# Turning V by VectorE and block transfers, and scoring wide rows in steps of 512 keys, in a fused attention and ternary layer

## What is computed

```
y = x * rsqrt(mean(x*x) + eps) * rms_w
q, k, v = split(y @ w_in.T)              # 32 q heads, 8 k heads, 8 v heads
q, k = rope(q), rope(k)
qk = q @ k.T / 8, causal mask, softmax
y = (attn @ v) @ w_out.T
x = layernorm(x + (x + y))
x_q = ternary(x); w = ternary(weight) + rram_variation
out = layernorm(x + x_q @ w.T)
```

## Time and profile before

| | us |
|---|---|
| median of 3 runs (lowest, highest) | 1446.98 (1443.99, 1448.08) |
| the profiled execution, its own time | 1443.82 |
| its span, first to last instruction | 1442.0 |
| PE busy (weight loads) | 1355.3 (1106.9) |
| DVE busy | 1117.4 |
| ACT busy | 1082.9 |
| POOL busy | 873.2 |

### The profile page before, as it was taken

The page is one execution under the profiler, slowest core; times in us unless marked ns, Lnnn a source line. Parts: engine busy times, 40 slices in busy tenths (PEclk is TensorE's granted clock), DMA queues, the critical chain, the costliest instruction groups (busy, mean ns, idle before and its releaser), DMA issues.

```text
span 1442.0 us, 24292 instructions
## 1 busy us (share of the span) xinstructions
PE 1355.3 (94%) x7296; PEld 1106.9 (77%) x7296; DVE 1117.4 (77%) x2519; ACT 1082.9 (75%) x2277; POOL 873.2 (61%) x846
## 2 busy tenths in 40 slices
PE   4789999999999999999999999999999999996896
PEld 3677787878878787888878787888878788785674
DVE  4677877877786878778787887778787787776997
ACT  4777778787787788778787878778787878775563
POOL 1456566475646656476646657376646667477866
PEclk9899999999999999999999999999999999999999
DMA  6001110111101111111101111111101111011011
GB/s 204 23 25 48 44 34 27 55 27 44 38 16 52 51 32 31 52 30 41 39 18 52 49 34 30 45 38 41 35 22 52 49 32 31 26 36 56 23 63 66
DMA packets 45154, 61.74 MB, mean 43 GB/s; under 512 B 10464, under 2 KB 27104, under 8 KB 45024
## 3 DMA queue, kind: packets, MB, share of 16 engines
q1 hardware_dynamic: 45024, 60.20, 14.2%
HBM read 34.74 MB, written 4.46 MB: 27 GB/s over the span
## 4 chain that ended last, share of the span: by engine, by line
PE 70%; DVE 12%; issue 6%; ACT 6%; DMA 2%; POOL 2%; SPq 1%; DVEq 0%; POOLq 0%; ACTq 0%
PE x L1078 17%; PE s L1066 15%; PE t L1112 13%; PE x L1096 9%; PE ot L1032 7%; PE ot L1030 7%; DVE prob_lo L997 3%; DVE prob L929 3%; ACT prob L766 2%; DMA spread<-recip_rows 1%; ACT prob_hi L737 1%; DVE stats L828 1%; PE x L1086 1%; ACT q_t L801 1%; DVE acc L990 1%
## 5 line engine op out<-in xcount | busy, mean ns | idle before, releaser
L997 DVE TENSOR_TENSOR prob_lo<-t,prob_hi 128x512 fp32r<-128x512 f32 x576 | 393.9, 686 | 95.5 <-ACT prob_hi L737 90.8
L737 ACT ACTIVATE prob_hi<-t 128x512 fp32r<-128x512 f32 x576 | 341.7, 594 | 167.6 <-PE t L1112 161.6
L929 DVE CUSTOM_DVE_ANT_0 prob<-s,mask 128x896 f32<-128x896 f32 (+7 forms) x512 | 382.0, 752 | 76.0 <-PE s L1066 63.0
L1066 PE MATMUL s<-k_t,q_t 128*128 128x512 f32 (+3 forms) x1536 | 385.1, 365 | 31.1 <-DVE neg_max L929 25.3
L766 ACT ACTIVATE prob<-prob,neg_max 128x896 f32<-128x896 f32 (+7 forms) x512 | 393.2, 769 | 22.3 <-DVE neg_max L929 20.1
L1112 PE MATMUL t<-ident,prob 128*128 128x128 f32 x2304 | 346.2, 273 | 2.0 <-ACT prob L766 2.0
L1112 PEld LDWEIGHTS t<-ident,prob 128*128 128x128 f32 x2304 | 286.4, 140 | 79.0 <-ACT prob L766 5.5
L1066 PEld LDWEIGHTS s<-k_t,q_t 128*128 128x128 f32 x1536 | 257.2, 191 | 87.4 <-DVE neg_max L929 46.0
L1030 PE MATMUL ot<-prob_hi,v_sb 128*128 128x512 f32 x576 | 242.9, 422 | 0.0
L1032 PE MATMUL ot<-prob_lo,v_sb 128*128 128x512 f32 x576 | 231.7, 402 | 11.2 <-DVE prob_lo L997 10.9
L710 POOL TENSOR_TENSOR o_lo<-o_raw,o_hi 128x256 fp32r<-128x256 f32 x128 | 94.6, 739 | 217.2 <-ACT o_hi L821 216.3
(11 more groups left out here) (86 smaller groups left out, 1949.9 us busy)
## 6 DMA issues: line engine op xcount, KB each, us to landing
swapped<-flat SPq DMA_DIRECT2D x320, 64.0 KB, 2.0
spread<-recip_rows SPq DMA_DIRECT2D x128, 128.0 KB
recip_rows<-turned SPq DMA_DIRECT2D x512, 0.5 KB
raw<-L_attn_w_in SPq DMA_DIRECT2D x8, 768.0 KB, 4.5
raw<-L_attn_w_out SPq DMA_DIRECT2D x8, 512.0 KB, 3.6
out<-acc SPq DMA_DIRECT2D x16, 256.0 KB, 2.0
acc<-L_attn_x SPq DMA_DIRECT2D x3, 1024.0 KB, 10.0
acc<-L_attn_x SPq DMA_DIRECT2D x4, 256.0 KB, 3.7
```

The lines of the kernel that those rows point to most:

```text
L737: act.activation(prob_hi[:, u % 2, :], t_ps[u % 2][:, :], ACT.Copy).then_inc(prob_hi_done, 1)
L929: dve.tensor_tensor_reduce(out=prob_row(s, h), in0=s_ps[:, off:off + cols], in1=mask[:, KEYS - cols:KEYS], scale=-DH ** -0.5, scalar=3e38, ...
L997: dve.tensor_tensor(prob_lo[:, u % 2, :], t_ps[u % 2][:, :], prob_hi[:, u % 2, :].bitcast(F32), ALU.subtract).then_inc(prob_lo_done, 1)
L1066: mm = pe.matmul(s_ps[:, off + c * P:off + c * P + cols], q_t[:, h, s * P:(s + 1) * P], k_t[:, part, keys:keys + cols], start=(part == 0), ...
```

## The change

- V is turned without TensorE. `vt` is now a VectorE instruction that turns `flat`'s rows 64 to 127 in blocks of 32x32 into `v_blocks` (SBUF, the upper half of a tensor `halves` whose lower half is `o_low`). A new event `vm` has SyncE issue eight DMAs of 32 partitions x 128 columns that bring the blocks to their places in `v_rows`. A new event `vh` has VectorE make the two parts of `v_sb` from `v_rows`. V uses no bank of `x_ps` any more, and the copy into `flat` waits for the block turn (`v_blocks_done`).
- Scores of rows of s >= 4 are made in steps of at most 512 keys, ordered by pairs of heads: (h, 0), (h + 1, 0), (h, 1), (h + 1, 1). Steps alternate between the two banks, and TensorE waits for the step before the last. The second step starts its minimum from the first one's (`low_max`).
- The tables have new numbers throughout; `stats` has two slots instead of four, and the DMA scratch size is 256 instead of 1024.

```diff
+SCORED = (0, 4, 8, 12, 16, 24, 32, 40, 48)
+def score_steps(s):
+    if s < HALF:
+        return [(h, 0) for h in range(HG)]
+    return [(h, c) for pair in (0, 2) for c in range(2) for h in (pair, pair + 1)]
...
+                        elif e[0] == "vm":
+                            hh = 2 * e[1] + e[2]
+                            wait(sp, v_blocks_done, g, 4, hh + 1)
+                            wait(sp, v_done, g, 4, hh)
+                            for a in range(2):
+                                for b in range(4):
+                                    sp.dma_start(v_rows[32 * b:32 * b + 32, a * P:(a + 1) * P],
+                                                 v_blocks[32 * a:32 * a + 32, b * P:(b + 1) * P]).then_inc(v_moved, 16)
...
                             if n % 3 == 2:
-                                wait(act, v_hi_done, g, 4, 2 * b + half + 1)
+                                wait(act, v_blocks_done, g, 4, 2 * b + half + 1)
...
-                            wait(dve, sc_full, g, 2 * NT * HG, kk * HG + h + 1)
-                            dve.tensor_tensor_reduce(out=prob_row(s, h), in0=s_ps[:, off:off + cols],
-                                                     in1=mask[:, KEYS - cols:KEYS], scale=-DH ** -0.5, scalar=3e38,
-                                                     op0=ALU.add, op1=ALU.min,
-                                                     accum_out=neg_max[:, kk % 4, h:h + 1]).then_inc(max_done, 1)
+                            wait(dve, sc_full, g, STEPS_MADE, n + 1)
+                            least = neg_max[:, kk % 4, h:h + 1] if c == s // HALF else low_max[:, h:h + 1]
+                            if c:
+                                wait(dve, max_done, g, STEPS_MADE, n - 1)
+                            dve.tensor_tensor_reduce(out=prob_row(s, h)[:, c * BANK:c * BANK + cols],
+                                                     in0=s_ps[:, off:off + cols], in1=mask[:, seen:seen + cols],
+                                                     scale=-DH ** -0.5, scalar=low_max[:, h:h + 1] if c else 3e38,
+                                                     op0=ALU.add, op1=ALU.min, accum_out=least).then_inc(max_done, 1)
...
                         elif e[0] == "vt":
                             _, b, half = e
+                            hh, n = 2 * b + half, chunk(b, half, 2)
+                            wait(dve, flat_done, g, CHUNKS, n + 1)
+                            wait(dve, v_moved, g, 4 * P, hh * P)
+                            dve.transpose(v_blocks.rearrange("p (b t j) -> p t b j", b=4, j=32),
+                                          flat[DH:P, n % 2, :].rearrange("p (t b i) -> p t b i", b=4, i=32)
+                                          ).then_inc(v_blocks_done, 1)
+                        elif e[0] == "vh":
...
+                            wait(dve, v_moved, g, 4 * P, (hh + 1) * P)
...
+                            dve.tensor_copy(hi, v).then_inc(v_hi_done, 1)
                             wait(dve, v_hi_done, g, 4, hh + 1)
+                            dve.tensor_tensor(lo, v, hi.bitcast(F32), ALU.subtract).then_inc(v_done, 1)
...
-                            wide = s >= 4 or s == 0 and h < 2
-                            wait(pe, max_done, g, 2 * NT * HG, n if wide or s == 4 and h == 0 else n - 1)
+                            wait(pe, max_done, g, STEPS_MADE, n - 1)
...
-                        elif e[0] == "vt":
-                            _, b, half = e
-                            n = chunk(b, half, 2)
-                            wait(pe, roped, g, CHUNKS, n + 1)
-                            for i in range(HALF):
-                                mm = pe.transpose(bank[:, i * P:(i + 1) * P], flat[:, n % 2, i * P:(i + 1) * P],
-                                                  ident[:, :])
-                            mm.then_inc(x_full, 1)
```

One line pair shows how the tables of a tile change (`MIDDLE`, first row of s = 4: places of the scores, the exponentials, `rc`, `rs`):

```diff
-        ((41, 50, 56, 60), (44, 58, 70, 72), 92, 137), ((74, 77, 88, 101), (88, 95, 102, 119), 116, 164),
+        ((41, 42, 48, 48, 56, 60, 64, 67), (52, 56, 73, 75), 129, 156),
```

More of the change, by code:

```diff
@@ L202, in body_plan @@
         scores, exps, norm, spread = at_pass["SCORES"][b * NT + s - 2]
-        for h in range(HG):
-            put(scores[h], ("sc", b, s, h))
+        for at, (h, c) in zip(scores, score_steps(s)):
+            put(at, ("sc", b, s, h, c))
         for h in range(HG):
@@ L213, in body_plan @@
                 put(at, (kind, b, half, c))
-        put(turn, ("vt", b, half))
+        for kind, at in zip(("vt", "vm", "vh"), turn):
+            put(at, (kind, b, half))
     if opening:
@@ L319, in seq_block @@
         prob_lo = sb("prob_lo", [P, 2, BANK], F32R)
-        o_low = sb("o_low", [DH, BANK])
+        halves = sb("halves", [P, BANK])
+        o_low = halves[0:DH, :]
+        v_blocks = halves[DH:P, :]
+        v_rows = sb("v_rows", [P, 2 * P])
         o_raw = sb("o_raw", [P, 2, P])
@@ L371, in seq_block @@
         table_in = [sem(f"table_in{n}") for n in range(2)]
+        v_blocks_done = sem("v_blocks_done")
+        v_moved = sem("v_moved")
         v_hi_done = sem("v_hi_done")
@@ L435, in wait_x_free @@
                 wait(eng, flat_done, g, CHUNKS, chunk(b - back, half, c) + 1)
-            elif kind == "vt":
-                wait(eng, v_done, g, 4, 2 * (what[0] - back) + what[1] + 1)
             elif kind == "op":
@@ L449, in chunk, with scored @@
             return 3 * (2 * b + half) + PLACE[c]
+        def scored(b, s, h=0, c=0):
+            return b * SCORED[NT] + SCORED[s] + score_steps(s).index((h, c))
+        STEPS_MADE = 2 * SCORED[NT]
         def unit_of(u):
@@ L762, in one @@
                             row = prob_row(s, h)
-                            wait(act, max_done, g, 2 * NT * HG, kk * HG + h + 1)
+                            wait(act, max_done, g, STEPS_MADE, scored(b, s, h, s // HALF) + 1)
                             wait(act, recip_done, g, 2 * NT, kk - 3)
@@ L797, in one @@
                             if c < 2:
-                                wait(act, sc_full, g, 2 * NT * HG, ((b - 1) * NT + HALF * (half + 1)) * HG)
+                                wait(act, sc_full, g, STEPS_MADE, (b - 1) * SCORED[NT] + SCORED[HALF * (half + 1)])
                                 act.activation(q_t[0:DH, 2 * c, at], x[0:DH, :], ACT.Copy)
@@ L802, in one @@
                             else:
-                                wait(act, sc_full, g, 2 * NT * HG, (b if half else b - 1) * NT * HG)
+                                wait(act, sc_full, g, STEPS_MADE, (b if half else b - 1) * SCORED[NT])
                                 for rows in (slice(0, DH), slice(DH, P)):
@@ L1053, in events @@
                         elif e[0] == "sc":
-                            _, b, s, h = e
-                            kk = b * NT + s
-                            n, off = kk * HG + h, s_bank(s, h)
-                            half = s // HALF
-                            wait(pe, parts_done, g, CHUNKS, chunk(b, half, h // 2) + 1)
-                            wide = s >= 4 or s == 0 and h < 2
-                            wait(pe, max_done, g, 2 * NT * HG, n if wide or s == 4 and h == 0 else n - 1)
-                            for c in range(0, s + 1, 4):
-                                cols = min(4, s + 1 - c) * P
-                                keys = k_slots(b, c // 4) * P
-                                for part in range(2):
-                                    mm = pe.matmul(s_ps[:, off + c * P:off + c * P + cols], q_t[:, h, s * P:(s + 1) * P],
-                                                   k_t[:, part, keys:keys + cols], start=(part == 0), stop=(part == 1))
+                            _, b, s, h, c = e
+                            n = scored(b, s, h, c)
+                            cols, off = min(BANK, (s + 1) * P - c * BANK), n % 2 * BANK
+                            keys = k_slots(b, c) * P
+                            wait(pe, parts_done, g, CHUNKS, chunk(b, s // HALF, h // 2) + 1)
+                            wait(pe, max_done, g, STEPS_MADE, n - 1)
+                            for part in range(2):
+                                mm = pe.matmul(s_ps[:, off:off + cols], q_t[:, h, s * P:(s + 1) * P],
+                                               k_t[:, part, keys:keys + cols], start=(part == 0), stop=(part == 1))
                             mm.then_inc(sc_full, 1)
```

51 lines of the change are left out of this document (26 added, 25 removed), and 141 rows, old and new, of tables (FIRST, LAYER, OUTPUT, PROJECT).

## The result

| | median, us (lowest to highest, runs) |
|---|---|
| before | 1447.85 (1443.99 to 1448.61, 5) |
| after | 1438.73 (1437.47 to 1441.06, 5) |
| after / before | 0.9946, 95% interval 0.9931 to 0.996 |

The changed kernel is faster by 9.1 us by the medians; the ratio of all runs, 0.9946, makes it 0.54%, 7.8 us. The forecast was 17.2 us, 1.2%: the sign and the range held, the size was twice too large. The profiled execution of before (1443.82) lies at the low end of its runs and that of after (1441.06) is the slowest of its own, so the two spans differ by less than 3 us. Terms are therefore compared by stretches of the traces, and totals by medians.

The account below looks back on a forecast made before the run. PE's own work was taken to bound the middle bodies, DVE the end. Terms -13.6 - 8 + 5 + 1.4 - 2 = -17.2 us, taken from the median 1446.98, gave 1430 us, range 1410 to 1446.

Parts of the forecast that it names:

- A: V's transposes leave TensorE: 31 groups at 0.44 us each, -13.6 us.
- about 161: Sign for the V turns leaving TensorE: a middle-body period of about 161 us in place of 163.1.
- B: Wide score rows no longer wait for the whole previous row: -8 us together.
- the 20 that was named: Sign for the score rows: PE's own wait for `neg_max` below 20 us.
- C: VectorE gets 95 us more work from split rows, block turns and V's subtraction; +5 us on the path.
- most of that has cover: VectorE's added 11.9 us a body mostly falls into its idle time; 1.4 us a body lies in full stretches.
- if V's split stalls beside GpSimd: One of the conditions under which the prediction called itself wrong; no size given.
- VectorE gives it all back: Rival, 9%: 22 of VectorE's 95 us land on the path in place of 5, gain gone, 1447 us.
- D: The end, where DVE sets the time: six wide rows split at 0.23 us each, +1.4 us.
- E: The start-up: the third copy to `flat` no longer waits for DVE to read V, -2 us.
- SyncE's queue: 256 added `vm` issues of 0.29 us, costed at nothing; as rival, 6%: they delay the reciprocals, +9 us, 1439.

Follow-up runs that it names:

- e1: The kernel before, with each of the 32 V turns on TensorE done twice: 1457.87 us, ratio 1.0078 to before.
- e3: The kernel before with the score steps of the change alone, at places derived from the old tables: 1543.96 us, ratio 1.0668 to before.
- e7: The changed kernel with the subtraction for V's low part moved from VectorE to GpSimd: 1427.73 us, ratio 0.9889 to before.
- e11: As e7, but with V's low part back on VectorE in the start-up and the opening body: 1424.33 us, ratio 0.9852 to before.
- e2: The kernel before with V's new path alone, at places derived from the old tables: 1516.52 us, ratio 1.048 to before.
- e5: The changed kernel with V's low part written as zeros by an instruction with one input: 1435.15 us, ratio 0.9931 to before.
- e6: The changed kernel with the second score step's minimum started from a constant, not from low_max: 1434.94 us, ratio 0.9929 to before.
- e10: The changed kernel with V's low part computed twice on VectorE: 1456.17 us, ratio 1.0074 to before.

## Why the prediction was right or wrong

**A, the turns leave PE (-13.6): right.** By e1 11 to 14 us. It is hidden in the changed kernel's period, not absent: with V's low part on GpSimd the period falls by 2.3 us, to 160.8, which is the "about 161" that was forecast.

**B, the banks (-8): the waits fell as said, the worth isn't measured.** PE's own waits for score rows fell by 12.1 us, to 13.2, under the 20 that was named; e3 could not price them.

**C, VectorE's load (+5): the step that failed.** The amount of load was put too low: added up from means, as the sum did it, the score steps brought 69 us, the block turn 23 and the dearer low part 24, 116 in place of 95. DVE's busy time rose by 72.0 only, because records overlap: in order of time a step of 512 columns and its read take 0.61 us to the next start, not 0.683 + 0.083:

```profile
678.77 0.68 DVE L962 CUSTOM_DVE_ANT_0 prob<-s,mask 128x512 f32<-128x512 f32 x1
679.38 0.08 DVE L962 DVE_READ_ACCUMULATOR2_ANT low_max<- 128x1 f32 x1
679.38 0.68 DVE L1040 TENSOR_TENSOR prob_lo<-t,prob_hi 128x512 fp32r<-128x512 f32 x1
```

What failed is the price of that load on the path, and in it the sentence "most of that has cover". The forecast charged V's low part at one place of four, in a full stretch, with 0.44 us of a total of 1.4, and put half of the 1.4 on the path: 0.7 us a body. The other low parts were taken as covered by VectorE's idle time. Measured, V's low part alone costs 2.3 us a period (e7): 0.6 us behind the one at 597.65, 0.9 around that at 636.29, and 0.85 behind that at 677.40, which lies in the wide stretch itself. It took 1179 ns in the mean and not 864, and an in-order queue holds `prob_lo` and the row minima behind it; idle time elsewhere in the stretch is no cover for that.

Taking the low part off VectorE gives back 8 to 13.5 us (e7, e11). That is the whole instruction; the 424 ns that it had before the change are in it, and the price of the excess alone wasn't measured. Nor does a run separate the blocking from the instruction's mere presence; for the blocking speaks that 27 of 32 ended with GpSimd's instruction. That the fourth place, just as long, costs nothing shows that it also takes somebody who waits: PE has no wait of its own there. As a remainder, with A at -11 to -14, B at -12 and nothing at the ends, the difference of -9 leaves +14 to +17 for C; by the profiled executions, which differ by less than 3 us, it would be some 6 more. The forecast's own sentence, "if V's split stalls beside GpSimd", names it: the stall was put into the busy time and not into the queue behind it.

This also bears out what was cited there. The same subtraction took 424 ns alone and 1401 in the median, but 426 in the median in e2, where GpSimd stood waiting for the reciprocals for 101 us. By the Trainium skill, SBUF — State Buffer, section Who interferes with whom, an instruction with two SBUF inputs or in a two-port mode and one of GpSimd exclude each other. The instruction of e5, with one input, was held in the same way (294 ns alone, 1263 in the median); that fits the second half, if it ran in such a mode, which no row names.

**The rival "VectorE gives it all back"** was given 9%. What happened is that mechanism at some two thirds: by the remainder, not by a run, some 15 us on the path where 22 would have cancelled the gain.

**D, the end (+1.4): not shown either way.** From the transposes of the last unit to the end 34.6 us in place of 35.4; the final body and the end together took 224.2 in place of 225.1. The gains of A and B in that body are in these figures too, and so is the clock, 0.98 against 1.00 between 1350 and 1430 us. VectorE stayed busy for 75.2 of those 80 us, as said.

**E, the start-up (-2): the sign is right, the size uncertain.** The third copy to `flat` came 1.2 us sooner (29.23 in place of 30.45), and the bodies began at 43.9 in place of 45.8 us. Single executions scatter as much: they began at 43.7 to 45.3 in the runs made from the changed kernel, and at 44.4 in e1. The opening body took 192.1 us in place of 190.7, but two stretches at 1.2 GHz lie in it that the kernel before doesn't have there; in e5 and e6, with one and none, it took 189.3 and 189.0.

**SyncE's queue (0):** the result was right for this kernel (PE's wait at the output projection fell from 6.3 to 5.5 us) and the price was wrong. An issue of `vm` took twice the 0.29 us of the sum:

```profile
L576 SPq DMA_DIRECT2D v_rows<-halves x256: 507/590/1661, 32.3 to 1280.8; - x128
```

The 0.29 came from the 0.5 KB issues of `recip_rows`. The kernel before had another row, of transfers over as many partitions as these, that would have said 0.59:

```profile
L554 SPq DMA_DIRECT2D swapped<-flat x320: 507/590/1748, 22.4 to 1293.3; - x160
```

## What to carry to other kernels

A unit of work taken off the bounding engine pays only as far as the second engine's deliveries keep up. Idle time in a stretch is not cover by itself: ask for each added instruction what stands behind it in its queue and who waits for that. Price an instruction by the least and the most of its kind, by what runs beside it, and not by the mean; where it competes with GpSimd for SBUF, GpSimd may be the better home for it (here 0.6 to 0.9% of the kernel's time). And a change that reorders a hand-made schedule can't be split into its parts at the old places: each part alone cost 5 or 7% here, both 10%, and with places made for them they gained. And before two single executions are compared, look at the granted clock of both.

## What the hardware showed that was not expected

- An instruction of VectorE that begins while one of GpSimd's runs can stand until that one is through: 27 of V's 32 low parts ended 0.28 us behind it, a one-input form (e5) 0.15 us behind it. One that began first wasn't held (426 ns in e2).
- A wait of TensorE can cost twice. In e10 PE waits 1.8 us for `prob_lo` at the same place in all six middle bodies; behind three of these waits it runs at 1.2 GHz for some 3 us, and those bodies take some 1.4 us more.
- The custom minimum instruction takes 62 ns more when its start value comes from SBUF than when it is a constant, at each of four widths (747 against 683 ns at 512 columns, 345 against 287 at 128).
- A copy from SBUF to SBUF of 256 columns took 286 ns in the median where the same from PSUM took 416; the subtraction, 424 at its least, was the same from either.
- GpSimd needed 0.74 us for the subtraction for which VectorE beside it took 1.18. The Trainium skill, Perfetto Trace Analysis, section Optimizing Scalar/DVE Operations, warns that moving work between these two might not help, as they share a read port. In e7 it did: 32 subtractions moved, 8 to 10 us won.
- Issuing a DMA took SyncE 0.59 us for 16 KB over 32 partitions, and 0.29 for 0.5 KB.
